# Splitting a routed tile's store, adding an unneeded gather, reordering the last additions, and cutting the frame loads at row 64

## What is computed

```python
# tokenizer: windows of 8 frames, stride 4 -> 93 slots of 640 values per clip
win = xp[:, idx, :].reshape(B, num_slices, NUM_FRAMES * D)
h = relu(win @ W1 + b1); h = relu(h @ W2 + b2)
h = batch_norm(h)                                  # over all 32*93 rows
h = h + attention(layernorm(h))                    # 16 heads of 64
x = layernorm(h)
out = h + x + shared_expert(x) + sum_over_top2(p_k * routed_expert_k(x))   # 8 routed experts, F = 1024
```

## Time and profile before

| what | value |
|---|---|
| median of three executions | 1033.21 us |
| the profiled execution, its own time | 1032.04 us |
| its span, first to last instruction | 1030.4 us |
| TensorE (PE) busy | 1008.5 us, 98% of the span |
| VectorE (DVE), ScalarE (ACT), GpSimd (POOL) busy | 641.6, 506.1, 424.5 us |
| mean granted TensorE clock | 0.998 of full |
| DMA traffic | 113.22 MB, mean 110 GB/s |

### The profile page before, as it was taken

How to read it: one execution, slowest core, us unless ns; L and a number is a source line. 1 busy time by engine, 2 the same in 40 slices (tenths; PEclk the granted TensorE clock), 3 DMA queues, 4 the chain that set the end, 5 groups by cost and what they waited for, 6 DMA issues and landing times. The chain is left out here.

```text
span 1030.4 us, 24361 instructions
## 1 busy us (share of the span) xinstructions
PE 1008.5 (98%) x8436; PEld 941.6 (91%) x8437; DVE 641.6 (62%) x1608; ACT 506.1 (49%) x1128; POOL 424.5 (41%) x541
## 2 busy tenths in 40 slices
PE   7998999999999999999999999999999999999997
PEld 7996898888989888898988899999999999999997
DVE  4666867878788787878867665343343344354565
ACT  3553454454545445454445564454454455445442
POOL 1001653254352625435252334325571555202886
PEclk9999999999999999999999999999999999999999
DMA  9725999921000100100011524324432424122564
GB/s 181 135 64 200 361 346 344 344 65 38 16 15 30 30 30 22 37 15 15 30 31 61 168 80 158 114 64 139 142 113 60 142 61 142 31 61 72 143 166 128
DMA packets 104084, 113.22 MB, mean 110 GB/s; under 512 B 29824, under 2 KB 94816, under 8 KB 104032
## 3 DMA queue, kind: packets, MB, share of 16 engines
q1 hardware_dynamic: 75388, 72.96, 23.3%
q0 software_dynamic: 17632, 27.02, 9.0%
q10 hardware_dynamic: 11012, 12.56, 3.8%
HBM read 49.43 MB, written 62.95 MB: 109 GB/s over the span
## 5 line engine op out<-in xcount | busy, mean ns | idle before, releaser
L1407 POOL TENSOR_TENSOR prob<-prob,rc 93x372 f32<-93x372 f32 x128 | 107.9, 845 | 238.1 <-DVE rc L1286 236.1
L989 PE MATMUL pj_ps<-xg,wA 128*128 128x372 f32 x768 | 164.3, 348 | 0.9 <-DVE xg L815 0.3
L1981 DVE TENSOR_TENSOR act_s<-sc_ps,act_s 128x384 fp32r<-128x384 f32 (+1 forms) x84 | 41.4, 494 | 161.6 <-ACT sc_ps L1823 160.3
L989 PEld LDWEIGHTS pj_ps<-xg,wA 128*128 128x128 f32 x768 | 125.3, 188 | 8.9 <-DVE xg L815 3.2
L1821 ACT ACTIVATE act_s<-sc_ps 128x384 fp32r<-128x384 f32 (+1 forms) x84 | 36.9, 439 | 148.3 <-PE sc_ps L1714 145.0
L975 PE MATMUL pj_ps<-wB,xg 128*93 128x512 f32 x384 | 102.0, 401 | 0.0
L1604 POOL DMA_INDIRECT raw<-y_rows,y_at x48 | 64.1, 1335 | 78.8 <-issue 77.9
L1728 PE MATMUL dn_ps<-wA,act_s 128*128 128x256 f32 x720 | 85.6, 279 | 0.0
L1728 PEld LDWEIGHTS dn_ps<-wA,act_s 128*128 128x128 f32 x720 | 83.5, 188 | 0.0
L1036 PE MATMUL y_ps<-wB,oT 128*128 128x256 f32 x576 | 78.0, 280 | 0.6 <-DVE oT L1290 0.6
L1148 ACT ACTIVATE qT<-pj_ps 128x372 f32<-128x372 f32 x64 | 30.8, 481 | 96.9 <-PE pj_ps L989 95.3
(11 more groups left out here) (228 smaller groups left out, 2106.3 us busy)
## 6 DMA issues: line engine op xcount, KB each, us to landing
slots<-zeros SPq DMA_DIRECT2D x8, 3072.0 KB, 23.4
y_rows<-zeros SPq DMA_DIRECT2D x5, 2688.0 KB, 21.0
rows_in<-slots SPq DMA_DIRECT2D x22, 384.0 KB, 3.4
y_rows<-rows_out ACTq DMA_DIRECT2D x22, 384.0 KB, 2.5
raw<-in_L_ffn_routed_up POOLq DMA_DIRECT2D x7, 1024.0 KB, 5.5
raw<-in_L_ffn_routed_down POOLq DMA_DIRECT2D x7, 1024.0 KB, 8.0
ln_out<-split SPq DMA_DIRECT2D x8, 744.0 KB, 3.2
sx<-ln_out ACTq DMA_DIRECT2D x5, 744.0 KB
```

What stands on the lines that cost most here:

```text
L989: ins = pe.matmul(pj_ps[:, t, 0:N], wA[:, wp, at:at + P], xg[:, dp, m, :], start=(k == 0), stop=(k == 5))
L1407: pool.tensor_tensor(p, p, rc[:, u % 2, :].unsqueeze(2).broadcast_to([TP, 4, SL]), ALU.mult).then_inc(scaled, 1)
```

## The change

It has four parts. (1) The frame loads are cut at row 64 in place of row 80, in all groups: bodies 0 to 63 and 64 to 92, edges 0 to 63 and 64 to 91. The memset of the padding covers partitions 64 to 93 only, and in group 0 the loads of rows 0 to 63 no longer wait for it. (2) After the last routed tile VectorE copies two thirds of `dn_ps` and ScalarE the last third, and ScalarE stores the two pieces with a DMA each. (3) GpSimd issues one gather from `slots`, whose rows nothing uses, and waits for it before it waits for the last store. (4) The last group's additions no longer wait for combinations; the combinations of chunks 21 to 23 wait for the additions instead, and chunks 19 and 20 are combined later.

```diff
-            def load_bodies(eng, g):
+            def load_bodies(eng, g, parts=((0, 64), (64, SL))):
                 s = g % 2
-                for lo, hi in ((0, 80), (80, SL)):
+                for lo, hi in parts:
                     eng.dma_start(frames[lo:hi, s, :, 0:KF], slots_of(g, lo, hi)).then_inc(x_in[s], 16)
             def load_edges(eng, g):
-                for lo, hi in ((0, 80), (80, SL - 1)):
+                for lo, hi in ((0, 64), (64, SL - 1)):
+                    if g == 0 and lo == 64:
+                        eng.wait_ge(edge_pad, 1)
...
+                load_bodies(sp, 0, ((0, 64),))
                 sp.wait_ge(edge_pad, 1)
-                load_bodies(sp, 0)
+                load_bodies(sp, 0, ((64, SL),))
...
-                act.wait_ge(edge_pad, 1)
                 load_edges(act, 0)
...
-                dve.memset(frames[:, :, :, (STRIDE - 1) * D:XW], 0.0).then_inc(edge_pad, 1)
+                dve.memset(frames[64:FG, :, :, (STRIDE - 1) * D:XW], 0.0).then_inc(edge_pad, 1)
...
-                pool.wait_ge(y_stored, 17 + (t0 + wide + narrow) * 16)
+                pool.wait_ge(scattered, 2 * NC * 16)
+                pool.indirect_dma_start(out=y_ring(YR - 1, 1), out_offset=None, in_=slots,
+                                        in_offset=bass.IndirectOffsetOnAxis(ap=slot_now[:, 0, 0:1], axis=0)
+                                        ).then_inc(ring_warm, 16)
+                pool.wait_ge(ring_warm, 16)
+                pool.wait_ge(y_stored, 33 + (t0 + wide + narrow) * 16)
...
+                pe.wait_ge(y_third, 1)
                 pe.wait_ge(y_out, 1 + t0 + wide + narrow)
                 down(wS, G1)
...
-                store_y(t0 + wide + narrow)
+                n_last = t0 + wide + narrow
+                act.wait_ge(rdn_done, 1 + n_last)
+                act.wait_ge(y_stored, 1 + n_last * 16)
+                act.activation(rows_out[:, 2, :], dn_ps[:, 1, 0:HD], ACT.Copy).then_inc(y_third, 1)
+                act.wait_ge(y_third, 1)
+                at = y_row(n_last)
+                act.dma_start(y_rows[bass.ds(at, WIDE), :].rearrange("(a p) n -> p a n", p=P)[:, 2, :], rows_out[:, 2, :]
+                              ).then_inc(y_stored, 16)
+                act.wait_ge(y_out, 1 + n_last)
+                act.dma_start(y_rows[bass.ds(at, WIDE), :].rearrange("(a p) n -> p a n", p=P)[:, 0:2, :], rows_out[:, 0:2, :]
+                              ).then_inc(y_stored, 16)
...
                 def add(g, c):
                     dve.wait_ge(dn_done, g * C + (c + 1))
-                    if g == LN and c < C - 1:
-                        dve.wait_ge(combined, LN * C + c + 1)
...
-                    dve.wait_ge(*((summed, b + 1) if b < LN * C or last else (kept, NG)))
+                    dve.wait_ge(summed, b + 1)
...
-                put_y(expert(E - 1))
+                n_last = expert(E - 1)
+                dve.wait_ge(rdn_done, 1 + n_last)
+                dve.wait_ge(y_stored, 1 + n_last * 16)
+                dve.tensor_copy(rows_out[:, 0:2, :].rearrange("p a n -> p (a n)"), dn_ps[:, 0, :]).then_inc(y_out, 1)
...
-                           G1 + 4: ((21,), (22,), (), (23,))}
-                during = {G1 + 4: {2: 18, 4: 19, 6: 20}}
+                           G1 + 4: ((20,), (21,), (22,), (23,))}
+                during = {G1 + 4: {2: 18, 7: 19}}
```

More of the change, by code:

```diff
@@ L1502, in audio_tower_kernel @@
             y_stored = sem(c, "y_stored")
+            y_third = sem(c, "y_third")
+            ring_warm = sem(c, "ring_warm")
             rows_ready = sem(c, "rows_ready")
```

## The result

| | before | after |
|---|---|---|
| median, lowest to highest (us) | 1031.16, 1029.28 to 1033.77 (6 runs) | 1056.95, 1055.74 to 1059.26 (6 runs) |
| ratio to before, 95% interval | | **1.0259** [1.0246, 1.0271] |
| profiled execution: own time, span, clock | 1032.04, 1030.4, 0.998 | 1057.22, 1055.6, 0.988 |

The account below looks back on a forecast made before the run. TensorE, busy 98% of the span, was taken as the bound, with the tokenizer becoming bound by one DMA engine: 21.4 - 0.4 = +21.0 on 1032.04 is 1053.0, with the median 1.2 higher 1054; range 1042 to 1080.

Parts of the forecast that it names:

- The bound and the mechanism of part 1: Tokenizer frame loads: 29 rows go to one DMA engine, whose 10.7 us period per group exceeds TensorE's 8.38.
- two readings: Frame loads: engines are the largest number up to 16 dividing the rows, or always 16 with an uneven last share.
- Its size: Frame loads: group 7 is there at 86.3 us instead of being turned at 64.91, +21.4 us in all.
- The clock: TensorE's waits can drop its clock: up to 3 us for the two halves behind group 7, left out of the sum.
- Part 2, the split store: After the last routed tile, copy and store split between VectorE and ScalarE: -0.4 us, bounds +0.3 to -0.9.
- what is left is its size, 256 KB for 384: Last tile's store: it leaves when it did before, but 128 KB less at 359 GB/s saves 0.37 us.
- Part 3, the gather: Unneeded gather in GpSimd's idle time: 0 us, as the pause belongs to the wait; bounds 0 to -0.8.
- Part 4: Order of the last additions: 0 us; TensorE's 1.10 us pause goes, but the last gather lands after its last matmul.
- The 29 rows are spread: Frame loads: an uneven share over 16 engines, so not slower, 1032 us (1029 to 1034); 15 in 100.
- It keeps up after the first group: Frame loads: one engine, but only groups 0 and 1 come late, +6 us, 1039; 3 in 100.
- Far slower: Frame loads: one engine at the crowded rate of 92 ns a piece, +58 us, 1091; 4 in 100.
- That the early issue saves nothing: Start: row 93's load still goes out after the memset, so nothing is saved; counted inside the spread-rows rival's range.

Follow-up runs that it names:

- experiment 3: The kernel before with only the body cut moved from row 80 to row 58 (58 and 35 rows): 1059.05 us, ratio 1.0285.
- experiments 1: The kernel before with only the body cut moved from row 80 to row 64 (64 and 29 rows): 1058.69 us, ratio 1.0277.
- 4: The kernel before with only the body cut moved from row 80 to row 38 (38 and 55 rows): 1041.71 us, ratio 1.0109.
- experiment 9: The kernel before with only the unneeded gather added ahead of the last store's wait: 1029.18 us, ratio 0.9990.
- 7: The kernel before with the split store and the new order of the last additions, without the unneeded gather: 1031.25 us, ratio 1.0012.
- 6: The kernel before with the split store, unneeded gather and new order of the last additions, frame loads as before: 1029.32 us, ratio 0.9996.
- experiment 5: The changed kernel with the bodies of groups 1 to 7 cut at row 80 again, only group 0 at 64: 1035.73 us, ratio 1.0060.

## Why the prediction was right, and where its sizes were off

**The bound and the mechanism of part 1: right.** TensorE had no slack in the tokenizer, so what starved it reached the end in full. Counting small packets left two readings of how rows go to engines, and the first holds: one engine for 29 rows, 2 for 58, and the dose follows the pieces on the busiest (132, 136 and 96: mean periods of 10.98, 11.22 and 9.08 us). The windows inside the waits show one engine at work, and two in experiment 3. (In the count of the earlier trace rows the 61 are exact if row 93 goes to 4 engines, not to 1 as I assumed, and it does: after sends group 5's 4 pieces of 960 B at 61.35, 61.41, 61.43 and, behind the bodies on the lone engine, 66.59 us. 16 + 13 + 16 + 12 + 4 = 61.) This agrees with what the Trainium skill, DMA: Bandwidth & Descriptors, section "Why a DMA increments its semaphore by 16 and not by 1", says of the number of engines. A load of 29 rows was not timed wholly by itself.

**Its size: low by 4.1 us**, 25.54 for 21.4. The rate of the engine by itself is not what was off: I took 57 ns a piece, which is the rate of 16 engines over 16, and alone it needs 55. The five periods from group 1 to 6 average 10.80 us for my 10.7. The miss is at the two ends. 1.6 us are there at the first transpose (12.98, forecast 11.4) and 2.1 by group 1 (24.22, forecast 22.1); 0.5 comes in the five periods and 1.5 in the last one, of 12.24 us. The last is the long one in experiments 1, 3 and 4 too (12.01, 12.61 and 10.82). What is different there is the weights. One part of 512 KB goes out behind each of the groups 1 to 6, two parts behind group 7, and the other engines carry them while the one is still at its pieces. A window of after:

```profile
84.00:88.60 4.60, 2.74 (x16) 2.42 (x14) 1.78 (x3) 1.14 (x2) 0.00 (x0) 1.00 1.03 217
```

Counted one by one in the trace, 60 pieces of 1280 B start from 83.5 to 88.6 us, one in 85 ns, and 32 from 72.8 to 75.3 us, beside the single part, one in 78 ns. So a piece is slower beside busy engines than alone, and my sum had no such term: it had 57 ns throughout and put the weights' 2.5 us on top. That this comes out right for five periods is in part luck; for the last one, with twice the weights, it is too low. Why group 0 lands 1.6 us late was not worked out.

**The clock: named and left out**, with up to 3 us. Behind group 7 it cost 1.64; what it cost earlier is hidden in the waits. The granted clock from 8 to 30 us is 0.69, where the kernel before has 0.92; and behind group 7's wait of 3.71 us it is 0.59, nearer the 1.2 than the 2.4 GHz level; the windows of after:

```profile
78.20:90.40 12.20, 8.53 (x54) 8.18 (x54) 5.46 (x11) 4.53 (x9) 0.00 (x0) 1.00 0.60 132
90.40:94.60 4.20, 4.15 (x18) 4.15 (x19) 1.40 (x3) 1.39 (x3) 0.00 (x0) 0.59 0.03 11
```

The period of that wait was still at full clock; the clock fell as the work resumed.

**Part 2, the split store: -0.4 forecast, not confirmed.** The copies and the issues came out as worked (0.69 for the copy, 1.10 us to the store's departure). What is not borne out is the step "what is left is its size, 256 KB for 384": the store of 256 KB took 2.9 to 4.0 us to land in the six kernels that have it, the whole one 3.0 to 3.6 in eight. A single execution moves by more than the 0.37 us that were forecast.

**Part 3, the gather: 0 forecast, about 1 us gained** (experiment 9; 1.6 between 7 and 6). The step that failed is the one from the earlier trace rows, that the pause belongs to the wait and nothing to a first use. That row is of scatters; with a gather 60 us before, the pause is 0.12 us shorter and the first gather 0.09, which is then the second of its kind, and 47 more are shorter by 10 ns. The bound of -0.8 lies inside the interval, 0.1 to 2.0.

**Part 4: 0 forecast, +0.5 [-0.4, +1.4] measured**, and by the mechanism that I gave: TensorE's pause is gone, and the end hangs on the last gather.

**The sum.** The difference of the spans is 25.2 for a forecast of 21.0. The 4.2 are 4.1 too little for the loads, 1.6 of clock, and at the end 2.0 gained for 0.4. Of these 2.0, part is the chance of one profile: the first gather came 5.03 us after the copy's start, for 5.71 before, and in the other kernels with the split store 5.5 to 6.1. In medians I was 3.0 too low, and 5.0 in their difference, since the kernel before, with the runs made beside the changed one, has 1031.16 for the 1033.21 on which I had built.

**The rivals.** "The 29 rows are spread" needed 1032 and a first transpose before 8.5; both fell. "It keeps up after the first group" is just what experiment 5 built, and it gave +6.2 where I had worked out +6; with all groups cut at 64, the period excludes it. "Far slower" would have had 92 ns throughout. I had held against it that nothing crowds the lone engine; in the stretches with weights something does (78 and 85 ns a piece), and elsewhere it is 55. That the early issue saves nothing is wrong as well: with the 29 rows cut in two, the first transpose comes 1.0 us earlier.

## What to carry to other kernels

Where a tile is loaded in two pieces, choose the cut by the row counts, not by where it is handy: the largest number up to 16 that divides each count is the number of engines, and a prime above 16 leaves one. Then compare the pieces on the busiest engine, times the time of one, and the other loads that pass meanwhile, with the consumer's period: here 132 pieces and the weights made 11 us where TensorE takes 8.4, while 28 + 1 or 16 + 13 cost one more DMA a group and no time that shows. In a profile the signs are a low DMA share beside waits for DMA, a share of 0.07 in the waits, and issues that hold their queue for microseconds.

## What the runs showed of the hardware

- One DMA engine by itself, with pieces of 1280 B from HBM, moved 23 GB/s (18 pieces in 1 us), as much as a sixteenth of the 359 that all 16 reached in the long window (22.4). Beside other engines at work on weights its pieces started one in 78 to 85 ns, for 55 alone.
- The issuing queue is held when a load has few engines: in after, two issues of bodies took 5.3 to 6.2 us for 0.80, and two of edges behind them 3.0 to 3.4 for 0.83 (groups 2 to 7). The attention weights behind group 6 went out 10.3 us after the first issue of that group, for 2.3 in the kernel before. The kernel before has this once, 3.80 us for the two issues at 9.78 us, when much else was on its way.
- Gathers of 124 rows on GpSimd went by their number: 1.40 us for the first, 1.31 for the second, 1.28 for the third, even with 57 us between. The pause behind the wait was 0.99 us with no gather ahead, 0.87 with one, 1.25 with two. The cause is open.
- VectorE's memset of 1152 columns took 1.02 us on 30 partitions and on 94.
